# Adding the offset lnx_b onto the bonus values with a TensorE product, and fetching the rows bf and lnf_w by a transfer of their own

## The reference, cut to what matters

```python
y = (y - mu) * jax.lax.rsqrt(var + 0.00064)
y = y * lnx_w.reshape(H, HEAD) + lnx_b.reshape(H, HEAD)
y = y + (r_ * k_ * r_k.reshape(H, HEAD)).sum(-1, keepdims=True) * v_
y = y.reshape(x.shape)
return y * g @ Wo
...
h = _layernorm(inp + att, norm_w, norm_b)
out = _layernorm(jax.nn.silu(h @ Wf + bf), lnf_w, lnf_b)
```

## Time and profile before

| What | us |
|---|---|
| Runs | 776.88, 230.71, 231.01 |
| Median of the runs | 231.01 |
| The profiled execution's own time | 230.83 |
| Its span in the profile | 229.1 |

### The profile page before, as it was taken

One profiled execution on the slowest core, in us unless ns is written; L12 is line 12 of the kernel. 1 busy time (PEld: TensorE's weight loads), 2 busy tenths in 40 slices (PEclk: granted clock), 3 DMA queues, 4 the chain that ended last, 5 costly groups with the idle time before them and its releaser, 6 DMA issues.

```text
span 229.1 us, 3195 instructions
## 1 busy us (share of the span) xinstructions
PE 220.0 (96%) x1192; PEld 167.7 (73%) x1192; DVE 166.0 (72%) x311; ACT 101.1 (44%) x196; POOL 93.4 (41%) x89
## 2 busy tenths in 40 slices
PE   8999999999999899999989999999999699999995
PEld 8998898889888688879474444444557488998963
DVE  2156387767579899981773484899988899698971
ACT  2256425375489497614145245597512202160310
POOL 5104203655566821971025616744863127330000
PEclk9999999999999999999999999999999999999999
DMA  6999859966968973099983298000000000000011
GB/s 235 429 412 399 358 185 451 393 263 215 379 235 318 413 322 137 0 342 419 429 313 150 78 339 363 0 0 0 1 0 3 0 0 3 0 0 4 0 43 49
DMA packets 6639, 43.99 MB, mean 192 GB/s; under 512 B 864, under 2 KB 1376, under 8 KB 1760
## 3 DMA queue, kind: packets, MB, share of 16 engines
q1 hardware_dynamic: 6480, 43.66, 48.2%
q10 hardware_dynamic: 144, 0.13, 0.2%
HBM read 43.27 MB, written 0.52 MB: 191 GB/s over the span
## 4 chain that ended last, share of the span: by engine, by line
PE 69%; DVE 26%; issue 2%; ACT 1%; DVEq 0%; POOL 0%; POOLq 0%
PE psum L412 49%; PE psum L454 16%; DVE ring_r L939 5%; PE psum L428 2%; DVE slots_r L1049 1%; PE psum L416 1%; DVE small L1042 1%; DVE slots L921 1%; DVE slots L1140 1%; ACT slots L1596 1%; PE psum L580 1%; DVE small L911 1%; DVE slots_r L1037 1%; DVE slots L927 1%; DVE psum L1063 1%
## 5 line engine op out<-in xcount | busy, mean ns | idle before, releaser
L412 PE MATMUL psum<-ring_r,slots_r 128*128 128x512 f32 x288 | 69.8, 396 | 2.0 <-DVE slots_r L1109 1.5
L412 PEld LDWEIGHTS psum<-ring_r,slots_r 128*128 128x128 f32 x288 | 53.0, 188 | 15.2 <-ACT slots_r L1596 2.1
L412 PE MATMUL psum<-ring,slots 128*128 128x512 f32 (+5 forms) x170 | 61.4, 513 | 0.7 <-DVE slots L1266 0.5
L1921 POOL TENSOR_TENSOR ring_r<-ring,ring_r 128x640 fp32r<-128x640 f32 x18 | 36.3, 2028 | 43.2 <-ACT ring_r L1596 43.1
L1596 ACT ACTIVATE slots<-psum 128x256 f32<-128x256 f32 (+4 forms) x48 | 20.7, 455 | 71.3 <-PE psum L412 32.4
L412 PEld LDWEIGHTS psum<-ring,slots 128*128 128x128 f32 (+1 forms) x170 | 29.3, 190 | 28.3 <-issue 25.5
L1596 ACT ACTIVATE ring_r<-ring 128x2048 fp32r<-128x2048 f32 x20 | 37.9, 1912 | 7.7 <-PE psum L412 6.8
L454 PE MATMUL psum<-slots,ring 128*128 128x128 f32 x320 | 37.5, 276 | 0.5 <-ACT slots L1596 0.5
L454 PEld LDWEIGHTS psum<-slots,ring 128*128 128x128 f32 x320 | 36.5, 192 | 1.2 <-ACT slots L1596 0.9
L939 DVE TENSOR_TENSOR ring_r<-ring,ring_r 128x1408 fp32r<-128x1408 f32 x18 | 30.2, 1692 | 2.5 <-ACT ring_r L1596 2.3
L1916 POOL TENSOR_TENSOR small<-small,mhalf 128x1 f32<-128x1 f32 x16 | 10.6, 663 | 36.0 <-DVE small L913 34.5
(11 more groups left out here) (184 smaller groups left out, 244.2 us busy)
## 6 DMA issues: line engine op xcount, KB each, us to landing
ring<-blocks SPq DMA_DIRECT2D x36, 1024.0 KB, 8.6
bc<-vecs SPq DMA_DIRECT2D x1, 3072.0 KB, 15.1
bc<-vecs SPq DMA_DIRECT2D x1, 1280.0 KB, 6.6
bc<-vecs SPq DMA_DIRECT2D x1, 512.0 KB, 13.7
slots<-xin SPq DMA_DIRECT2D x1, 256.0 KB, 5.2
y<-slots SPq DMA_DIRECT2D x1, 256.0 KB, 2.0
y<-slots SPq DMA_DIRECT2D x2, 128.0 KB, 1.8
slots<-xin ACTq DMA_DIRECT2D x1, 128.0 KB, 2.7
```

The costliest lines, as they stand in the source:

```text
L412: return t.matmul(o_, l, r, start=first, stop=last)
L1921: g.tensor_tensor(ring_r[:, p, CUT:], ring[:, p, CUT:], ring_r[:, high(name), CUT:], ALU.subtract).then_inc(*split_lowg.inc(name))
```

## The change

`bonus(b)` is gone from DVE. In its place PE adds lnx_b onto `v_p[b]` after ACT's multiplication, by one product with 64 rows (`lift(b)`): `lift(0)` stands between step 1r and step 1v, `lift(1)` behind step 1g. DVE's last add waits for the new flag `lifted` and reads v_p from PSUM; the other operand now lies in pv. The vector lnx_b gets its rounded part and its rest in the partitions 64 to 127 of the slot that holds bf: one more `row_high` on ACT and one more `low_row` on DVE. bf and lnf_w come by a transfer of their own, issued between f1 and rk, behind a wait for the layer norm x1 of both sequences; the late transfer brings the other three vectors.

```diff
-        row_parts = {"a0": (W0, 0), "w0": (A0, 64), "bf": (FREE, 0)}
+        row_parts = {"a0": (W0, 0), "w0": (A0, 64), "bf": (FREE, 0), "lnx_b": (FREE, 64)}
...
             fetch("f1")
+            s.wait_ge(*normed[0].at("x1"))
+            s.wait_ge(*normed[1].at("x1"))
+            eng.dma_start(bc[:, 0:2, :], spread(FIRST_BC, FIRST_BC + 2)).then_inc(s_bf, 16)
             fetch("rk")
...
-            eng.dma_start(bc[:, 0:len(BCAST) - FIRST_BC, :], spread(FIRST_BC, len(BCAST))).then_inc(s_bc2, 16)
+            eng.dma_start(bc[:, 2:len(BCAST) - FIRST_BC, :], spread(FIRST_BC + 2, len(BCAST))).then_inc(s_bc2, 16)
...
+            def lift(b):
+
+                i, p = row_parts["lnx_b"]
+                s.wait_ge(*by_a[b].at("pv"))
+                s.wait_ge(*rows_v.at("lnx_b"))
+                t.matmul(v_p[b], share[p:p + 64, :], bc_r[p:p + 64, i, :], start=False, stop=True,
+                         skip_group_check=True).then_inc(*lifted[b].inc("v"))
...
             step(1, "r", 3, 4, wait=turned[1].at("n4"))
+            lift(0)
             step(1, "v", 4, 5, wait=evict[1].at("k"))
...
             step(1, "g", 5, 6, wait=rk_v[1].at("km"))
+            lift(1)
             s.wait_ge(*rk_v[0].at("yg"))
...
-            def bonus(b):
-
-                s.wait_ge(*by_a[b].at("pv"))
-                v.tensor_tensor(pv[b], v_p[b], vec("lnx_b"), ALU.add).then_inc(*rk_v[b].inc("pv"))
-
...
             def norm_s(b):
-                s.wait_ge(s_bc2, 16)
+                s.wait_ge(s_bf, 16)
...
             low_row("bf")
+            low_row("lnx_b")
...
-            v.tensor_tensor(y_p[0], vc[0], y_p[0], ALU.mult).then_inc(*rk_v[0].inc("y"))
-            bonus(0)
+            v.tensor_tensor(pv[0], vc[0], y_p[0], ALU.mult).then_inc(*rk_v[0].inc("y"))
             s.wait_ge(*rk_v[0].at("y"))
-            s.wait_ge(*rk_v[0].at("pv"))
-            v.tensor_tensor(ys[0], y_p[0], pv[0], ALU.add).then_inc(*rk_v[0].inc("yb"))
+            s.wait_ge(*lifted[0].at("v"))
+            v.tensor_tensor(ys[0], pv[0], v_p[0], ALU.add).then_inc(*rk_v[0].inc("yb"))
...
-            bonus(1)
             s.wait_ge(*own_v.now())
             v.tensor_tensor(y_p[1], y_p[1], vec("lnx_w"), ALU.mult).then_inc(*own_v.inc())
             s.wait_ge(*own_v.now())
             s.wait_ge(*rk_g[1].at("rs"))
-            v.tensor_tensor(heads(y_p[1]), heads(y_p[1]), over(rs8[1], 64), ALU.mult).then_inc(*own_v.inc())
+            v.tensor_tensor(heads(pv[1]), heads(y_p[1]), over(rs8[1], 64), ALU.mult).then_inc(*own_v.inc())
             low_halves(0, "yg", T16_r, 0.5)
-            s.wait_ge(*rk_v[1].at("pv"))
+            s.wait_ge(*lifted[1].at("v"))
             s.wait_ge(*own_v.now())
-            v.tensor_tensor(ys[1], y_p[1], pv[1], ALU.add).then_inc(*own_v.inc())
+            v.tensor_tensor(ys[1], pv[1], v_p[1], ALU.add).then_inc(*own_v.inc())
...
-            row_high("bf", (s_bc2, 16))
+            row_high("bf", (s_bf, 16))
+            row_high("lnx_b", (s_bc1, 16))
```

More of the change, by code:

```diff
@@ L236, in build @@
         s_x, s_x0b = [sem("s_x0"), sem("s_x1")], sem("s_x0_right")
-        s_cols, s_bc0, s_bc1, s_bc2 = (sem(n) for n in ("s_cols", "s_bc0", "s_bc1", "s_bc2"))
+        s_cols, s_bc0, s_bc1, s_bc2, s_bf = (sem(n) for n in ("s_cols", "s_bc0", "s_bc1", "s_bc2", "s_bf"))
         s_y = [sem("s_y0"), sem("s_y1")]
@@ L256, in build @@
         x_sum = flags("x_sum", [], ["n4"])
-        rows_v = Flag(sem("rows_dve"), ["w0", "a0", "bf"])
+        rows_v = Flag(sem("rows_dve"), ["w0", "a0", "bf", "lnx_b"])
         rest_v = Flag(sem("rest"), ["rest"])
         mixed_v = Flag(sem("mixed_dve"), ["k", "a", "r", "v"])
-        rk_v = flags("rwkv_dve", ["vc", "c", "km", "ys", "ss", "e", "sb", "y", "pv", "yb", "yg"], ["c", "km", "rn",
-                     "ys", "c3", "c1", "sb", "vc", "c2s", "ss", "e", "pv", "yg"])
+        rk_v = flags("rwkv_dve", ["vc", "c", "km", "ys", "ss", "e", "sb", "y", "yb", "yg"], ["c", "km", "rn",
+                     "ys", "c3", "c1", "sb", "vc", "c2s", "ss", "e", "yg"])
         gates_v = flags("gates_dve", ["gl", "mask", "w"])
@@ L265, in build @@
         out_v = flags("out_dve", ["ms1", "ms0", "1", "0", "2", "fin"], ["ms0", "ms1", "0", "1", "2", "fin.a", "fin"])
-        rows_a = Flag(sem("rows_act"), ["share", "w0", "a0", "bf"])
+        rows_a = Flag(sem("rows_act"), ["share", "w0", "a0", "bf", "lnx_b"])
         turned = flags("turned", TURNS0, TURNS[1:])
@@ L304, in build @@
                      "r", "v", "g", "ro", "rf", "fg", "fq", "fk"])
+        lifted = flags("lifted", ["v"])
         score = flags("score", ["0", "1", "2", "3"])
```

## The result

The changed kernel takes 232.91 us (median of 6 runs, 231.78 to 233.08); the kernel before, run beside it, 230.86. The ratio is 1.006, with a 95% interval of 1.0035 to 1.0086: slightly slower. That is 1.0 us above the forecast of 231.9, at the very end of the range of 230.6 to 232.9. The 6 runs lie in two groups, two at 231.78 and 231.93 and four at 232.81 to 233.08. The profiled execution took 233.00 us, and its span is 231.2 us against 229.1.

A forecast was written before the change was run, and what follows sets the result against it. PE and DVE were both taken as nearly tight at the change, the chain running through DVE, then PE. Terms 0 + 0 + 0.97 us on 230.83 gave 231.80, from the median 231.98; forecast 231.9 us, range 230.6 to 232.9.

The forecast's parts named there:

- Parts 1 and 2: Early transfer of bf and lnf_w, and lnx_b's extra rounding on ACT and subtraction on DVE: hidden, cost 0.
- Part 3: lift(0) behind step 1r: DVE's add into ys[0] waits for it, so read_keys(1) and what follows come 0.97 us later.
- Parts 3 and 4: lift(0) before 1v and lift(1) behind step 1g cost PE 0.43 us each before the turning of yg(0).
- Part 5: bonus(1) gone: DVE wins 0.46 us before gated(1), but PE is later by 0.7 at yg(1)'s turning, so nothing gained.
- Part 6: End of the stretch: POOL's deviation for h moves 0.97 us to 170.50, with PE's 0.86 beside it, not added.
- A: Rival at the lifts: DVE isn't held, only PE's products cost, 0.7 us through ro(1) and h, 231.5 us; chance 0.13.
- B: Rival at lift(0): done by 151.64, so read_keys(1) isn't delayed; not slower, 230.7 us; chance 0.12.
- C: Rival at the early transfer: not hidden, delays the last context blocks 1.3 us, PE waits, 233.1 us; chance 0.05.
- D: Rival at the lifts: weight prefetch breaks or the result comes late, shift 1.5 us, 232.3 us; chance 0.11.

The follow-up runs named there:

- e6: Changed kernel with POOL's split of c00 put ahead of its ln3_b add at 68 us; median 231.82 us, ratio 1.0013.
- e4: Kernel before with only the early transfer of bf and lnf_w, no lift; median 231.52 us, ratio 1.0007.
- e5: Kernel before with POOL's split of c00 put ahead of its ln3_b add at 68 us; median 230.8 us, ratio 0.9984.
- e1: Changed kernel with sequence 1 as before: lift(0) only, bonus(1) back on DVE; median 231.48 us, ratio 1.0042.
- e2: Changed kernel with sequence 0 as before: lift(1) only, bonus(0) back on DVE; median 231.42 us, ratio 1.0008.
- e3: Changed kernel with DVE's add of sequence 0 moved behind the last operation POOL's power waits for; median 231.8 us, ratio 1.0045.
- e8: e6 without lift(0), lift(1) behind yg(0)'s turning, POOL's deviation for h ahead of its last rf split; median 231.18 us, ratio 0.9992.
- e11: Kernel before with one more, long satisfied wait on DVE ahead of the first norm_s; median 230.6 us, ratio 0.9989.
- e12: e10 with one more, long satisfied wait on DVE, as in e11; median 230.19 us, ratio 0.9964.
- e10: e5 with POOL's deviation for h first, then a wait for DVE's affine step, then the last rf split; median 230.77 us, ratio 0.9988.

## Why the prediction was right, point by point

The mechanism of the forecast holds in the stretch; that the measured 232.91 falls at the end of the range is luck. The loss measured between the medians is 2.05 us, twice the forecast 0.97, and the half that the forecast doesn't have, the late landing and the lock at 68 us, was in no term and no rival. The forecast was 231.9 us, and where the lock is out the changed kernel takes 231.82 (e6). The profiled execution's 233.00 is, but for 0.01, the sum's 231.80, the 1.14 us before the stretch, and 0.05 in it. Set against the subtraction, and so free of the 1.14:

| us after the subtraction | forecast | changed kernel |
|---|---|---|
| the add into ys[0] | 20.32 | 20.39 |
| read_keys(1) | 20.92 | 21.00 |
| POOL's power | 29.95 | 30.01 |
| turning of yg(0) | 31.50 | 31.77 |
| turning of yg(1) | 35.4 | 35.53 |
| POOL's deviation for h | 38.20 | 38.27 |
| the rf piece | 48.29 | 48.34 |

- **Parts 1 and 2, cost 0: right.** e4 shows the transfer free in the stretch, e6 beside e5 ahead of it: rk is issued at 83.52 against 83.51, the subtraction starts at 132.24 against 132.21. The rows of lnx_b went where the forecast put them: ACT's two roundings follow without a wait for a transfer, and DVE's two rests lie ahead of 2.34 us of idle time, in the changed kernel's rows of ACT and DVE:

```profile
134.91 1.26 ACT L1604 ACTIVATE bc_r<-bc 64x512 fp32r<-64x512 f32 x2
...
139.04 1.40 DVE L1131 TENSOR_TENSOR bc_r<-bc,bc_r 32x512 fp32r<-32x512 f32 x2
142.79 0.69 DVE L1443 TENSOR_REDUCE small<-slots 128x8 f32<-128x512 f32 x1 [2.34 <-ACT slots L1604]
```

- **Part 3, the hold on DVE, 0.97: right.** It measured 1.05 at read_keys(1). The lift lasts 0.49 and 0.50 in every trace, so the row of the bf product was the right one. The formula of the Trainium skill that was weighed there (0.38 us; "TensorE: Matmul & The Clock Gate", section Single matmul latency) is stated for a bf16 product over 128 rows; these are products in PE's short form of float32 over 64 rows, so they neither bear it out nor refute it.
- **Parts 3 and 4, what a lift costs PE: mis-sized.** The forecast took 0.43 us each, 0.86 together; it is 0.63 (e1) and 0.52 (e2), and 1.14 for both at the turning of yg(0) (31.77 less 30.63). The reason stood unread in the earlier trace rows: from 1r's last record at 151.57 to the bf product at 155.53 there are nine steps, 3.96 us, where 9 x 0.43 is 3.87; and the 16 records behind that product take 7.13 us, where 15 x 0.43 + 0.59 is 7.04. So the way into a short product costs 0.09 more and the way out of it as much again. lift(0) pays both, 0.61 worked out so; lift(1), behind which no step but the turning follows, pays the first, 0.52.
- **Part 5: right.** From line 1522 to line 1524 it is 0.73, as forecast, and gated(1) begins 34.49 us after the subtraction, against a forecast of 34.44. The turning of yg(1) waits for no engine: the second instruction taken from DVE paid nothing.
- **Part 6: right in what was last, lucky in the margin.** "With PE's 0.86 beside it and not on top" holds, as e1 alone gives the whole 1.05. But the forecast compared POOL's deviation at 170.50 with `out_o(0)`'s statistics at about 169.4, 1.1 us earlier, and left out two steps that DVE does between the statistics and the affine step, `low_halves(1, "yg")` and the centring. The changed kernel's rows of DVE, the second of them the centring:

```profile
170.75 0.65 DVE L1123 SCALAR_TENSOR_TENSOR slots_r<-psum,slots_r 128x512 fp32r<-128x512 f32 x1
171.31 0.74 DVE L935 SCALAR_TENSOR_TENSOR slots<-psum,small,bc 128x512 f32<-128x512 f32 x1
```

  The centring ends 0.22 us before POOL's result (172.05 against 172.27). So PE's products, over ro(0) and `out_o(0)`, reach h with 0.95, next to POOL's 1.02, and e3 won next to nothing.
- **Rivals.** A named the right second cause, PE's cost, but priced it at 0.7 and led it over ro(1); e3 shows 0.96, over ro(0) and `out_o(0)`. So A and the forecast could not have been told apart by the time of the changed kernel, only by the rows. B fell: read_keys(1) is late. C fell: no engine waits for a transfer between 75 and 110 us in the changed kernel's rows, and e5 and e6 reach the subtraction together. D fell: the lift shows no latency beyond its 0.50, and PE goes on 0.42 and 0.43 after it.

Open: why the block lands 0.3 us later in some executions; what share of runs loses the lock (5 of 23 to 15 of 33 for the same kernel), and whether the early transfer raises that share (20 of 40 against 7 of 31 beside it), which would be a cost of the change in the median; and why a place in DVE's list costs 0.46 us.

## What to carry to other kernels

Moving an instruction from a busy engine to another pays only if the new result is there when the old engine comes to it: here DVE gave up 0.60 us of work and stood 1.78 us for PE. Before taking the loss for the change's own, find the first instruction whose start differs between the two traces; if it lies ahead of the change, measure from a common event behind it. And when an edit that removes a cause gains nothing, look for a second chain that is late by nearly as much, as ro(0) and `out_o(0)` were in e3, and follow it over all engines: a row without a stated wait, like PE's at 172.94 there, can still be held, here by an affine step that had ended 0.05 us before.

## What the runs showed of the hardware

- Two elementwise instructions with both inputs in SBUF, one on DVE and one on POOL, don't overlap: 1.65 became 2.49 on DVE, 1.27 became 2.68 on POOL, 0.75 became 1.38 on DVE (e8). Where the two starts are 0.1 to 0.3 us apart, as at 68 us, which one loses differs from execution to execution, and with the late landing that turns the order it made two groups of runs 1.1 us apart.
- One extra wait on DVE, met at once, removed 0.46 us of idle time some 40 recorded instructions further on (from about 178 to 206 us), and made the end of the kernel, from the rf piece on, 0.35 to 0.4 us shorter (e11 against before, e12 against e10). Of 14 traces, the 7 with this instruction at its old place in the list have the idle time and the 7 with it one place further on have not; other places weren't tried, and no run shows what in the chip does it.
- A product over 64 rows between float32 products costs PE 0.52 to 0.63 us, though it lasts 0.50 and the next start comes 0.43 later.
